# Where the matmul operands stand in SBUF: one remainder of 2048 bytes for all of them

## What is computed

```
x = layernorm(x + causal softmax attention, 16 heads)            # layer 0
x = layernorm(x + ffn0(x))   # ternary weights 512->2048->512, gelu, 4-bit fake quantization
x = layernorm(x + linear attention, 16 heads, relu and decay)    # layer 1
x = layernorm(x + ffn1(x))   # 512->2048->512, gelu, float16 roundings between
```

## The kernel before, in words

| stage | matmul | before | after |
|---|---|---|---|
| 1 | `xT` with `w` | 672, 672 | 640, 640 |
| 2 | `kst` with `qst`; `probs` with `v` | 704, 704 | 640, 640 |
| 2 | `probs` with `ones` | 704, 64 | 640, 0 |
| 3 | `o` with `w` | 704, 704 | 640, 640 |
| 4 | `tern` with `xT`, `tern` with `h` | 672, 768 | 640, 640 |
| 4 | transposes, `x1` with `ident` | 704, 128 | 640, 128 |
| 5 | `la_w` with `aT` | 2016, 640 | 640, 640 |
| 5 | `wo` with `aT` | 640, 640 | 640, 640 |
| 5 | `kv` with `qT` | 896, 640 | 896, 640 |
| 6 | `w0` with `xT`, `w1` with `h` | 640, 640 | 640, 640 |

## Time and profile before

### The profile page before, as it was taken

How to read it: one execution, slowest core, us unless ns; L and a number is a source line. 1 busy time by engine, 2 the same in 40 slices (tenths; PEclk the granted TensorE clock), 3 DMA queues, 4 the chain that set the end, 5 groups by cost and what they waited for, 6 DMA issues and landing times. The chain is left out here.

```text
span 2633.3 us, 39827 instructions
## 1 busy us (share of the span) xinstructions
PE 2435.7 (92%) x12833; PEld 1800.0 (68%) x12833; DVE 1221.1 (46%) x2498; ACT 818.4 (31%) x1371; POOL 903.7 (34%) x1092
## 2 busy tenths in 40 slices
PE   7999699999999968599999996899999979999997
PEld 5888455555555536478888885688888768888886
DVE  3333477777777749701211113767766371111121
ACT  3222055555555541044444442101101112222221
POOL 0000155555555535323333333516243122222211
PEclk9999699999999988899999998899999989999999
DMA  6665735455445335410101102221312051000000
GB/s 246 225 223 193 182 84 135 108 120 132 108 120 132 77 111 176 157 40 17 64 32 63 62 19 84 96 94 66 110 49 96 31 191 40 32 32 32 32 33 32
DMA packets 154489, 255.29 MB, mean 97 GB/s; under 512 B 9648, under 2 KB 47536, under 8 KB 153904
## 3 DMA queue, kind: packets, MB, share of 16 engines
q1 hardware_dynamic: 137712, 208.20, 26.5%
q0 software_dynamic: 6144, 25.17, 2.9%
q10 hardware_dynamic: 10560, 20.97, 2.3%
HBM read 161.50 MB, written 92.27 MB: 96 GB/s over the span
## 5 line engine op out<-in xcount | busy, mean ns | idle before, releaser
L737 DVE CUSTOM_DVE_ANT_0 p_junk<-psum,p_causal 128x896 bf16<-128x896 f32 (+7 forms) x512 | 370.6, 752 | 159.8 <-PE psum L597 149.8
L700 ACT ACTIVATE p_probs<-psum 128x512 f32<-128x512 f32 (+1 forms) x640 | 331.3, 554 | 325.9 <-PE psum L608 320.6
L1149 POOL TENSOR_TENSOR p_h_lo<-p_h,p_h_hi 128x512 fp32r<-128x512 f32 x128 | 165.1, 1290 | 338.3 <-ACT p_h_hi L1178 338.3
L608 PE MATMUL psum<-p_qst,p_kst 98*128 98x512 f32 (+3 forms) x768 | 246.0, 384 | 17.2 <-ACT p_probs L700 10.9
L608 PEld LDWEIGHTS psum<-p_qst,p_kst 98*128 98x128 f32 x768 | 131.4, 190 | 170.8 <-ACT p_probs L700 84.8
L520 POOL TENSOR_SCALAR_AFFINE_SELECT p_probs<-p_probs 128x128 f32<-128x128 f32 x512 | 146.0, 306 | 264.8 <-ACT p_probs L700 263.8
L597 PE MATMUL psum<-p_kst,p_qst 96*128 96x512 f32 (+5 forms) x768 | 205.8, 369 | 20.8 <-DMA p_kst<-k_parts 17.3
L1802 POOL CAST p_h<-p_h 128x512 fp32r<-128x512 f16 x128 | 92.6, 723 | 373.1 <-ACT p_h L1826 373.1
L846 PE MATMUL psum<-p_xT_hi,tern 128*128 128x512 f32 x512 | 206.4, 403 | 1.4 <-DVE p_xT_lo L1248 1.4
L1217 PE MATMUL psum<-tern,p_h_hi 128*128 128x512 f32 x512 | 203.0, 397 | 2.1 <-POOL p_h_lo L1149 2.1
L846 PE MATMUL psum<-p_xT,p_w_hi 128*128 128x512 f32 x512 | 204.0, 398 | 0.7 <-ACT p_xT L1813 0.7
(11 more groups left out here) (184 smaller groups left out, 4639.8 us busy)
## 6 DMA issues: line engine op xcount, KB each, us to landing
p_qst<-q_parts SPq DMA_DIRECT2D x96, 256.0 KB, 4.5
p_kst<-k_parts SPq DMA_DIRECT2D x96, 256.0 KB, 6.8
q_parts<-p_qk_out SPq DMA_DIRECT2D x32, 512.0 KB, 2.8
k_parts<-p_qk_out SPq DMA_DIRECT2D x32, 512.0 KB, 2.7
ffn_x<-x SPq DMA_DIRECT2D x12, 1024.0 KB, 5.6
p_x<-in_x_t POOLq DMA_DIRECT2D x8, 1024.0 KB, 6.4
p_raw<-in_f_w POOLq DMA_DIRECT2D x8, 1024.0 KB, 8.0
v_rows<-p_v_out SPq DMA_DIRECT2D x32, 256.0 KB, 4.9
```

The source lines that it names most:

```text
L608: mm = pe.matmul(ST_BANKS[st % 2][:, col:col + CH - q0], kst[s][0:KD + 2, g, j * P:(j + 1) * P], qst[s][0:KD + 2, c, g, q0:CH], start=True ...
L700: act.activation(probs[:, n % 2, g, col:CH], ST_BANKS[st % 2][:, col:CH], ACT.Exp, scale=SM_SCALE).then_inc(p_ready, 1)
L737: dve.tensor_tensor_reduce(halves_of(junk[:, which, 0:n]), scores, halves_of(causal[:, SEQ - n:SEQ]), 1.0, FLOOR, ALU.add, ALU.max, rowmax ...
L1149: pool.tensor_tensor(h_lo[:, m % 2, :], h[:, m % 2, :], f32(h_hi[:, m % 2, :]), ALU.subtract).then_inc(hl_done, 1)
```

## The change

Nothing is computed otherwise, and each engine has the same instructions in the same order. Only addresses differ. `w_max` and `alpha` are taken from the right end, which needs 32 bytes each. A buffer `level`, which nothing reads or writes, follows there; its size is what is left of the distance between the lower and the upper end by 2048, so that the upper end then has the lower end's remainder, 640. In stage 4 `p4_b1` is allocated behind the operands instead of in front of them.

```diff
+LINE = 2048
...
 def phase_ffn0(nc, psum, ident, tern, kept, alpha, b1, b2, x1, x1_dram, y_dram, y_stored, after):
...
-        b1c = sb("p4_b1", [P, HT], F32)
         b2r = sb("p4_b2", [P, D], F32)
         xT_hi = sb("p4_xT_hi", [P, 2, KT, CH], F32R)
         xT_lo = sb("p4_xT_lo", [P, 2, KT, CH], F32R)
         h = sb("p4_h", [P, 2, CH], F32)
         h_hi = sb("p4_h_hi", [P, 2, CH], F32R)
         h_lo = sb("p4_h_lo", [P, 2, CH], F32R)
+        b1c = sb("p4_b1", [P, HT], F32)
...
 def build_program(...):
         ident = build_constants(nc, ctx)
+        few = lambda n, s: ctx.enter_context(nc.sbuf_tensor(n, s, F32, side="right"))
+        w_max, alpha = few("w_max", [P, 2]), few("alpha", [P, 2])
+
+        few("level", [P, (nc.sbuf_top - nc.sbuf_base) % LINE // 4])
         with ExitStack() as layer0:
             sb = lambda n, s, d: layer0.enter_context(nc.sbuf_tensor(n, s, d))
-            w_max = sb("w_max", [P, 2], F32)
...
             kept = sb("kept", [P, 2, 8, KT * HID // 64], F32)
-            alpha = sb("alpha", [P, 2], F32)
```

## The result

| | before | after |
|---|---|---|
| median, 4 runs each | 2634.29 us (2633.34 to 2635.98) | 2611.73 us (2611.02 to 2613.73) |
| span of the profiled execution | 2633.3 us | 2612.0 us |
| mean granted TensorE clock | 0.965 | 0.965 |

The ratio is 0.9915, 95% interval 0.9898 to 0.9932: the changed kernel is 22.6 us faster; forecast were 20.9 us less, 2613.3 us.

The account below looks back on a forecast made before the run. Bound in stages 4 to 6: PE's matmuls times their pitch, slow where operands' remainders differ. Stage 4's 13.3 plus stage 5's 7.6 make 20.9 us less, from 2634.18 to 2613.3 us; range 2608 to 2621 (about 0.85).

Parts of the forecast that it names:

- Stages 4, 5 and 6 are matmuls times pitch: Stages 4 to 6: PE's time is matmul count times pitch; the faster pitch gains 13.3 us in stage 4, 7.6 in 5.
- The deduction of 0.1 us a chunk: Stage 4: matmuls after transposes that miss the fast pitch, 0.1 us a chunk, 0.8 us in all, taken off the gain.
- The cover of the chain in stage 4: Stage 4: gelu, rounding and subtraction end 0.64 us before PE needs the result; the shorter step leaves 0.53 us.
- the rival of coinciding operands: Stage 4: all engines' operands at one remainder stretch the subtraction; at 2.15 us the time would be 2655 us; chance 0.03.
- 0 us for stages 1 to 3, with 2 us about stage 2: Stages 1 to 3: a shift that both operands share costs nothing, 0 us, with 2 us to either side for stage 2.
- The clock at the borders, 0 us with 3 to either side: Borders into stages 5 and 6: half-clock stretches may end sooner or later, 1.5 us each; 0 taken, 3 us either side.
- The remainder of 2048: Table of remainders: streams with both operands at one remainder run at 227 ns, those with them apart at 234 ns.
- Operands that multiply each other: Stages 1, 2, 3 and 6: operands that multiply each other keep their distance, so these stages change by 0 us.
- something else sets the 234 ns: Stages 4 and 5: other engines' load or whatever goes with la_w sets the pitch; time stays 2634.2 us; chance 0.08.
- only one of the two gains: Stage 4 or stage 5 alone gets faster: 2620.9 us (stage 4) or 2626.6 us (stage 5); chance 0.04.
- the first rival: Stages 4 and 5: something other than operand distance sets the 234 ns; time stays 2634.2 us; chance 0.08.

Follow-up runs that it names:

- e3: Changed kernel with 1248 bytes put behind ident, so all operands stand at common remainder 1888 instead of 640: 2613.34 us, ratio 0.9921.
- e5: Changed kernel with only stage 4's xT_lo and h_lo 96 bytes behind the common remainder and la_w_lo 96 before it: 2626.66 us, one execution.
- e10: Changed kernel with stage 6's w1 and h both 96 bytes further (736), w0 and xT left at 640: 2620.27 us, one execution.
- e1: Changed kernel without the filler: stage 4's operands at 640, la_w_hi and la_w_lo at 1952 against aT at 640: 2619.88 us, ratio 0.9947.
- e2: Kernel before plus a filler ahead of the right-hand buffers, la_w at 640 like aT, stage 4 still 672 and 768: 2626.79 us, ratio 0.9969.
- e7: Changed kernel with distances of 256 bytes in stage 4, 32 in stage 5 (la_w), 96 in stage 6: 2633.01 us, one execution.

## Why the prediction was right, point by point

- *Stages 4, 5 and 6 are matmuls times pitch*: right. 2048 shorter pitches gave 12.9 us of stage 4, 13.3 forecast; 1152 gave 7.2 us of stage 5, 7.6 forecast. Each was also measured alone, with 14.0 and 8.2 us of time (intervals 9.8 to 18.4 and 5.0 to 11.1 us, by the ratios).
- *The deduction of 0.1 us a chunk*: right in cause and size. It is the settling after transposes. In the changed kernel the 1975 pitches under 300 ns of stage 4 are 1.03 us longer in all than at 226.7 ns each, 0.13 us a chunk; in stage 6 it is 0.71 us, 0.09 a chunk. In the kernel before the 1978 pitches of stage 4 lie 13.86 us above the same measure, and 13.86 - 1.03 = 12.8 us is nearly all of the 12.9 us that the stage got shorter.
- *The cover of the chain in stage 4*: 0.53 us forecast. After, the subtraction starts at 1194.26, and its result is needed at 1196.08:

```profile
1192.73 0.78 ACT L1171 ACTIVATE p_h<-psum,p_b,alpha 128x512 f32<-128x512 f32 x1 [2.18 <-PE psum L847]
1193.55 0.63 ACT L1179 ACTIVATE p_h_hi<-p_h 128x512 fp32r<-128x512 f32 x1
1194.26 1.28 POOL L1150 TENSOR_TENSOR p_h_lo<-p_h,p_h_hi 128x512 fp32r<-128x512 f32 x1 [2.35 <-ACT p_h_hi L1179]
```

  1196.08 - 1195.54 = 0.54 us. So the rival of coinciding operands fell as well: over its 128 executions the subtraction takes 1283 ns on average, with 1290 before, though all stands at one remainder.
- *0 us for stages 1 to 3, with 2 us about stage 2*: right, stage 2 is 0.3 us shorter. The reason given, that a common shift costs nothing, is e3's result.
- *The clock at the borders, 0 us with 3 to either side*: right. The borders into stages 5 and 6 last 15.8 us each after, 15.8 and 15.9 before, and the clock granted over the 21 us into stage 6 is 0.51 in both.
- *The remainder of 2048*: the prediction took it from the table as it was, and the table cannot tell 2048 from 256; here it was wrong. What must agree is the remainder of 256. It cost the forecast nothing, since operands that agree by 2048 agree by 256, and that is luck, as no row of before that was read tells the two apart. This also explains what looked like chance: stage 4 (96 apart) and `la_w` (1376 apart) showed the same 233.8 ns because 1376 is 5 x 256 + 96.
- *"Operands that multiply each other"*: too narrow. By e5 and e10 everything in one run of matmuls must agree, the neighbours included. That did no harm to the number either, as the change brings all of them in stages 4 to 6 to one remainder.
- *The rivals*: "something else sets the 234 ns" is refuted by e1, e2 and e7, in which 227 and 234 ns follow the addresses into every stage; "only one of the two gains" by e1 and e2. The slow scores of stage 2, given for the first rival, fit the settling, as said above.
- *The forecast is 1.6 us above the measured median.* Only 0.4 us of it is in the profiled executions: a span of 2612.4 us was forecast and 2612.0 measured, since the two stages gained 0.8 us less than said and the rest of the span 1.2 us more than the zero put to it. The two errors partly cancel. The other 1.2 us is the scatter of executions: the profiled one of the changed kernel lies 2.0 us above its median, where the forecast assumed 0.8 as before.

## What to carry to other kernels

Where TensorE is the bound with long runs of float32r matmuls of 512 columns (the only ones that these runs tried), compare the distance of their starts between stages: a few ns more at the same shape and clock can be the addresses alone. Put all operands of such a run, streamed and loaded, at one remainder of 256 bytes; a filler of at most 224 bytes, or small buffers behind the large ones instead of in front, does it. The mixed short groups of the attention here gained nothing. The whole was worth 0.9% of this kernel.

## What the runs showed of the hardware that had not been expected

- Weights and streamed operand at different remainders of 256 bytes cost 4.6 to 6.7 ns a float32r matmul of 512 columns (2 to 3% of 227 ns); of 32, 64, 96 and 128 bytes 64 costs least and 96 most, and 256, 512 and 1280 cost nothing.
- The cost isn't local. With `la_w_lo` alone displaced, its neighbours with agreeing operands are slow too (231 to 234 ns), and groups of eight that agree within themselves but not with one another run at 230 to 232 ns on average, in the uneven sequence that otherwise follows transposes.
- After transposes a run of agreeing matmuls itself begins with two, five, six or nine uneven pitches (224 to 236 ns, apart from the first always the end of the same sequence) before it stays at 227. It costs about 0.1 us a chunk in stages 4 and 6.
